# A graph network layer on one core: p from centred weights and the transposed accumulator, x loaded in 32x32 pieces, blocks in place of rows

## What is computed

```python
def reference(x, adj, L0_gnn_evals, L0_gnn_t, L1_gnn_W, L1_gnn_b):
    # L0: spectral filter
    t_eff = jnp.clip(t[0], 1e-08, None)
    x_spec = jnp.einsum('nk,nc->kc', adj, x)
    coefs = jnp.exp(-evals * t_eff)[:, None]
    out = jnp.einsum('nk,kc->nc', adj, coefs * x_spec)
    x = _layernorm(x + out, axis=-1)
    # L1: graph convolution
    adj_hat = adj + jnp.eye(N)
    deg = jnp.sum(adj_hat, axis=1, keepdims=True)
    out = (adj_hat / deg) @ (x @ W) + b
    return _layernorm(x + jnp.tanh(out), axis=-1)
```

## Time and profile before

| what | value |
|---|---|
| median of 3 runs (lowest, highest) | 615.78 us (615.32, 616.95) |
| the profiled execution, its own time | 615.71 us |
| its span, first to last instruction | 613.9 us |
| TensorE matmul busy | 579.9 us, 94% |
| VectorE busy | 511.1 us, 83% |
| ScalarE busy | 399.2 us, 65% |
| GpSimd busy | 378.2 us, 62% |
| moved by DMA | 174.67 MB, mean 285 GB/s |

### The profile page before, as it was taken

How to read it: one execution, slowest core, us unless ns; L and a number is a source line. 1 busy time by engine, 2 the same in 40 slices (tenths; PEclk the granted TensorE clock), 3 DMA queues, 4 the chain that set the end, 5 groups by cost and what they waited for, 6 DMA issues and landing times.

```text
span 613.9 us, 7999 instructions
## 1 busy us (share of the span) xinstructions
PE 579.9 (94%) x2460; PEld 447.1 (73%) x2460; DVE 511.1 (83%) x572; ACT 399.2 (65%) x855; POOL 378.2 (62%) x223
## 2 busy tenths in 40 slices
PE   5999999999998999989999999999999979899993
PEld 5888888888875656758888788887888856656561
DVE  4799999999898988888899799696776768989992
ACT  4999999999996746356555654555444635554552
POOL 0000000000147878788999999879887898997892
PEclk9999999999999999989999999999999999999997
DMA  8999999999999999799979999296995499999101
GB/s 306 408 409 408 410 408 409 409 410 407 410 271 346 328 330 341 212 259 269 242 209 260 254 305 272 66 256 192 256 258 142 123 342 347 348 339 316 35 18 52
DMA packets 125065, 174.67 MB, mean 285 GB/s; under 512 B 6884, under 2 KB 105700, under 8 KB 125032
## 3 DMA queue, kind: packets, MB, share of 16 engines
q1 hardware_dynamic: 72608, 121.68, 59.2%
q10 hardware_dynamic: 52424, 52.58, 30.6%
HBM read 172.13 MB, written 2.11 MB: 284 GB/s over the span
## 4 chain that ended last, share of the span: by engine, by line
PE 60%; POOL 22%; DVE 9%; DMA 3%; issue 3%; ACT 2%; ACTq 1%; DVEq 0%; POOLq 0%
POOL lo L483 18%; PE ps L833 9%; PE ps L835 9%; PE ps L834 9%; PE ps L861 8%; PE ps L863 8%; PE ps L862 8%; PE ps L857 7%; DVE vt L690 5%; DMA raw<-in_adj_dram 2%; DVE lo L697 2%; POOL rstd L462 2%; PE ps L818 1%; ACTq L368 1%; POOL raw L476 1%
## 5 line engine op out<-in xcount | busy, mean ns | idle before, releaser
L483 POOL TENSOR_TENSOR lo<-vt,hi 128x1024 fp32r<-128x1024 f32 x126 | 317.6, 2546 | 31.8 <-ACT hi L538 31.2
L690 DVE STREAM_TRANSPOSE vt<-raw 128x1024 f32<-128x1024 f32 x184 | 222.0, 1226 | 63.1 <-PE ps L863 52.1
L538 ACT ACTIVATE hi<-vt 128x1024 fp32r<-128x1024 f32 x159 | 165.8, 1060 | 128.6 <-DVE vt L690 104.6
L671 DVE TENSOR_TENSOR lo<-raw,hi 128x1024 fp32r<-128x1024 f32 x124 | 156.3, 1265 | 19.1 <-ACT hi L524 10.2
L524 ACT ACTIVATE hi<-raw 128x512 fp32r<-128x512 f32 x256 | 158.9, 623 | 7.2 <-PE ps L835 4.0
L436 POOL TENSOR_TENSOR lo<-raw,hi 128x1024 fp32r<-128x1024 f32 x4 | 10.2, 2556 | 170.7 <-ACT hi L524 170.7
L861 PE MATMUL ps<-hi,s_hi 128*128 128x512 f32 x224 | 94.5, 422 | 7.6 <-POOL lo L483 5.7
L833 PE MATMUL ps<-hi,xg_hi 128*128 128x512 f32 x256 | 100.2, 392 | 1.5 <-DVE lo L671 1.4
L834 PE MATMUL ps<-lo,xg_hi 128*128 128x512 f32 x256 | 99.6, 389 | 0.0
L835 PE MATMUL ps<-hi,xg_lo 128*128 128x512 f32 x256 | 99.6, 389 | 0.0
L861 PE MATMUL ps<-hi,p_hi 128*128 128x512 f32 x206 | 88.1, 428 | 6.9 <-POOL lo L483 6.9
(11 more groups left out here) (69 smaller groups left out, 537.5 us busy)
## 6 DMA issues: line engine op xcount, KB each, us to landing
raw<-in_adj_dram SPq DMA_DIRECT2D x63, 1024.0 KB, 14.3
raw<-in_adj_dram SPq DMA_DIRECT2D x90, 512.0 KB, 9.7
raw<-in_adj_dram ACTq DMA_DIRECT2D x88, 512.0 KB, 11.8
late_raw<-in_adj_dram SPq DMA_DIRECT2D x8, 512.0 KB, 12.6
late_raw<-in_adj_dram ACTq DMA_DIRECT2D x8, 512.0 KB, 14.5
xn<-in_x_dram SPq DMA_DIRECT2D x8, 256.0 KB, 14.0
x_sb<-in_x_dram SPq DMA_DIRECT2D x8, 256.0 KB, 13.7
out_dram<-x_sb ACTq DMA_DIRECT2D x7, 256.0 KB, 2.9
```

The source lines that it names most:

```text
L483: nc.gpsimd.tensor_tensor(lo[:, slot(p), :], vt[:, slot(p), :], hi[:, slot(p), :].bitcast(f32), ALU.subtract).then_inc(pool_lo_ready, 1)
L538: nc.scalar.activation(hi[:, slot(s), :], vt[:, slot(s), :], ACT.Copy).then_inc(hi_ready, 1)
L671: nc.vector.tensor_tensor(lo[:, q % RING1, :], raw[:, k, 2 * h:2 * h + 2, :].rearrange("p r n -> p (r n)"), hi[:, q % RING1, :].bitcast(f3 ...
L690: nc.vector.transpose(vt[:, slot(s), :].rearrange("p (m a i) -> p m a i", m=2, a=RB), load_buffer(st.load).rearrange("p (a m e i) -> p e m ...
```

## The change

1. **Weights.** `centre` = identity - 1/128 is made on GpSimd, TensorE multiplies it with W, and VectorE copies the result (V, W with each column's mean taken off) over `w_sb`, all ahead of stage 1. The transposes of the identity that nobody reads go from 36 to 20. TensorE now waits for W's load and for `centre` ahead of them, and VectorE for `centred` ahead of its first split of x.
2. **p.** Since layernorm only takes off the mean and scales, p = rstd * (h @ V). The ending becomes: since -3, VectorE turns x in 32x32 blocks into `stage[:, 1]`; since 0, VectorE adds it to acc2(g) into `stage[:, 0]` (h transposed), in place of ScalarE's copy; since 1, TensorE turns this (4); since 2, ScalarE copies h to x_sb; since 3, VectorE makes statistics, mean and variance together, and TensorE multiplies `stage[:, 0]` by V (4); since 6, ScalarE makes p_hi with the scale rstd, in four pieces; since 7, VectorE makes p_lo in four pieces; since 8, ScalarE normalises x_sb in place (x1) and makes `full`. The turning of x1 by TensorE and its copy by ScalarE are gone.
3. **x.** A group's x comes in four DMAs of 32 partitions, in pieces of 128 B, where it was one DMA in pieces of 2 KB.
4. **Blocks.** x_sb, 1/deg and the result are laid out in blocks as p is. The sums come back in four DMAs with pieces of 128 B, and VectorE turns them once. A result goes out in four DMAs a group, in pieces of 512 B, half of them issued by SyncE and half by ScalarE.

```diff
+    PHI = 6
-    x_v = x.rearrange("(u a e h r) c -> u e a h (r c)", u=NU, e=2, h=QP // R, r=R)
+    x_v = x.rearrange("(u a e i) (b c) -> u e b i a c", u=NU, e=2, i=QP, b=QN)
+    out_v = out.rearrange("(u q m e i) c -> u e m q i c", u=NU, q=QN, m=JB, e=2)
...
-                    sp.dma_start(x_sb[:, g, :], x_v[g // 2, g % 2]).then_inc(x_in[g % 2], 16)
+                    for b in range(QN):
+                        sp.dma_start(x_sb[b * QP:(b + 1) * QP, g, :].rearrange("i (a c) -> i a c", c=QP),
+                                     x_v[g // 2, g % 2, b]).then_inc(x_in[g % 2], 16)
...
             def ending2(g, since):
-                if since == 1:
-                    act.wait_ge(mm_done, END2[g] + 1)
-                    nc.scalar.activation(stage[:, 0, :], acc2(g), ACT.Copy).then_inc(acc_out, 1)
-                if since == 7:
-                    normalise(acc2(g), g % 2, g, g, rs2, x1_ready)
-                if since == 9:
-                    act.wait_ge(x1T_done, g + 1)
...
+                if since == 2:
+                    act.wait_ge(accT_done, g + 1)
+                    nc.scalar.activation(x_sb[:, g, :], acc2(g), ACT.Copy).then_inc(h_ready, 1)
+                if since == PHI:
+                    act.wait_ge(pw2, g + 1)
+                    act.wait_ge(hw_done, g + 1)
+                    for m in range(JB):
+                        last = nc.scalar.activation(p_hi[:, blocks(g, m)], acc2(g)[:, m * C:(m + 1) * C], ACT.Copy,
+                                                    scale=rstd[:, g % 2, m:m + 1])
+                    last.then_inc(phi_ready, 1)
+                if since == PHI + 2:
+                    normalise(x_sb[:, g, :], g % 2, g, g, rs2, x1_ready)
...
+            dve.wait_ge(centred, 1)
+            nc.vector.tensor_copy(w_sb[:, :], ps[:, NK - 2, :P]).then_inc(wc_ready, 1)
...
-                if since == 2:
-                    dve.wait_ge(accT_done, g + 1)
-                    dve.wait_ge(x_in[par], 16 * (g // 2 + 1))
-                    nc.vector.tensor_tensor(acc2(g), acc2(g), x_sb[:, g, :], ALU.add).then_inc(h_ready, 1)
+                if since == -3:
+                    dve.wait_ge(x_in[par], 16 * QN * (g // 2 + 1))
+                    nc.vector.transpose(stage[:, 1, :], x_sb[:, g, :]).then_inc(xT_ready, 1)
+                if since == 0:
+                    dve.wait_ge(mm_done, END2[g] + 1)
+                    dve.wait_ge(xT_ready, g + 1)
+                    if g:
+                        dve.wait_ge(hw_done, g)
+                    nc.vector.tensor_tensor(from_blocks(stage[:, 0, :]), by_block(acc2(g)), by_block(stage[:, 1, :]),
+                                            ALU.add).then_inc(hT_ready, 1)
...
-            for _ in range(36):
+            pe.wait_ge(w_in, 16)
+            pe.wait_ge(centre_ready, 1)
+            nc.tensor.matmul(ps[:, NK - 2, :P], centre[:, :], w_sb[:, :], start=True, stop=True).then_inc(centred, 1)
+            for _ in range(20):
                 nc.tensor.transpose(ps[:, NK - 1, :P], ident[:, :], ident[:, :])
             pe.wait_ge(coef_ready, 1)
+            pe.wait_ge(wc_ready, 1)
...
                 if since == 1:
-                    pe.wait_ge(acc_out, g + 1)
-                    for r in range(R):
-                        last = nc.tensor.transpose(acc2(g)[:, r * C:(r + 1) * C], spread(stage[:, 0, :], r), ident[:, :])
+                    pe.wait_ge(hT_ready, g + 1)
+                    for m in range(JB):
+                        last = nc.tensor.transpose(acc2(g)[:, m * C:(m + 1) * C], stage[:, 0, m * P:(m + 1) * P],
+                                                   ident[:, :])
                     last.then_inc(accT_done, 1)
-                if since == 8:
-                    pe.wait_ge(x1_ready, g + 1)
...
```

More of the change, by code:

```diff
@@ L246, in spectral_then_graph_conv @@
         ident = sb("ident", [P, P])
+        centre = sb("centre", [P, P])
         w_sb = sb("w_sb", [P, C])
@@ L303, in parts3, with blocks @@
             return [(range(R // 2), ps[:, bank, :], row + 1), (range(R // 2, R), ps[:, LATE3[0], :], row + 2)]
+        def blocks(g, m):
+            return slice((g * JB + m) * C, (g * JB + m + 1) * C)
         def columns(rows):
@@ L369, in load_quarters, with store @@
                               adj_q[ld.group // 2, ld.group % 2, ld.wide, q]).then_inc(block_in[ld.buf], 16)
+        def store(eng, row, count, odd):
+            g = ENDINGS[row]
+            for m in [ms for ms, _, n in parts3(row) if n == count][0][odd::2]:
+                eng.dma_start(out_v[g // 2, g % 2, m], x_sb[:, g, m * C:(m + 1) * C]).then_inc(stored, 16)
         blk = ctx.enter_context(nc.Block())
@@ L416, in _ @@
                     sp.wait_ge(deg_out, 16)
-                    for h in range(NG):
-                        sp.dma_start(rdeg[:, h, :], deg_by_group[h // 2, h % 2]).then_inc(deg_in, 16)
+                    for q in range(QN):
+                        sp.dma_start(rdeg_tile[q * QP:(q + 1) * QP].rearrange("p g r -> p (g r)"), deg_by_block[q])\
+                            .then_inc(deg_in, 16)
+            for row in range(NG):
+                for _, _, count in parts3(row):
+                    sp.wait_ge(out_ready, count)
+                    store(sp, row, count, 0)
         @blk.gpsimd
@@ L630, in ending3 @@
                         act.wait_ge(out_ready, count)
-                        act.dma_start(out_v[g // 2, g % 2][:, :, columns(rows_of)], x_sb[:, g, columns(rows_of)])\
-                            .then_inc(stored, 16)
+                        store(act, row, count, 1)
             for p in range(AHEAD, POSITIONS):
@@ L775, in ending3 @@
                 if since == 2:
-                    dve.wait_ge(deg_in, 16 * NG)
+                    if row == 0:
+                        dve.wait_ge(deg_in, 16 * QN)
+                        nc.vector.transpose(rdeg[:, :, :, :].rearrange("p u m e -> p (u m e)"),
+                                            rdeg_tile[:, :, :].rearrange("p g r -> p (g r)")).then_inc(deg_s, 1)
+                        dve.wait_ge(deg_s, 4)
                     for rows_of, bank, count in parts3(row):
@@ L932, in ending3 @@
                             pe.wait_ge(out_ready, ENDINGS.index(0) + 1)
-                        for r in rows_of:
-                            last = nc.tensor.transpose(bank[:, r * C:(r + 1) * C], spread(stage[:, row % 2, :], r),
+                        for m in rows_of:
+                            last = nc.tensor.transpose(bank[:, m * C:(m + 1) * C], stage[:, row % 2, m * P:(m + 1) * P],
                                                        ident[:, :])
                         last.then_inc(sumT_done, 1)
-            pe.wait_ge(w_in, 16)
             for p in range(AHEAD, POSITIONS):
```

77 lines of the change are left out of this document (41 added, 36 removed).

## The result

| | before | after |
|---|---|---|
| median (lowest, highest), 6 runs each | 616.37 us (613.65, 618.59) | 631.86 us (628.36, 632.24) |
| ratio, with its 95% interval | | 1.0245 (1.022 to 1.0271) |
| span of the profiled execution | 613.9 us | 630.2 us |
| x alone undone (runs below; before 615.53 us in these) | | 620.48 us |
| x and the stores undone | | 611.59 us |

The change makes the kernel slower by 15.5 us. The forecast was 611.2 us with a range to 617.5: wrong in its sign. What it said of two kinds of DMA, x in pieces of 128 B (+1.7) and the stores (-0.1), was wrong by some 10 and 9 us.

A forecast was written before the change was run, and what follows sets the result against it. TensorE was taken as the bound, except from 285 to 348 us, where GpSimd's subtractions set the pace. Ten terms from -1.65 to +1.7 summed to -4.5, so 615.7 became 611.2 us, range 606.5 to 617.5.

The forecast's parts named there:

- x in pieces of 128 B: Group 0: small pieces make SyncE's queue 7.7 us later, load 4 lands at 218.4, GpSimd's chain starts 1.65 later: +1.7.
- in group 1 ... VectorE's and GpSimd's slack there covers: Group 1: SyncE's queue is late again by some 2 to 3 us at load 8, covered by slack.
- Later groups: 0: Groups after 1: 7.7 us more of queue time just fits, or the sums' return saves 4.6 us: 0.
- The end: Last results go out on two queues, and the sums come back in 128 pieces for 1024: -0.1 us.
- The start: Stage 1: with 20 transposes for 36, the first matmul comes at about 12.9 for 14.06, and this lasts: -1.15 us.
- Addition ahead of the transposes: Group endings: TensorE's transposes wait for VectorE's addition, 2.0 us in group 1, 0.9 in group 5, 0.2 in group 0.
- Mean and variance, the pause, the clock: Group 1: mean and variance 1.0 us earlier, pause before step 40 shrinks, clock stays up: about -1.65.
- the clock in the 4 us behind the new wait: Behind TensorE's new wait in group 1: clock at 1.00 means the forecast, at 0.5 rival C, 1.3 more.
- rival C: Chance 0.20: clock falls in group 1 (+1.3), VectorE's work costs up to 1, half-clock stays at group 7 (+0.7): 614.2 us.
- p, the other groups, VectorE's 8.4 us "hidden": VectorE's added 8.4 us costs 0; groups 0: -0.9, 3: +0.1, 4: -0.4, 5: -0.4, 6: -0.5, 7: -1.2.
- D: Chance 0.11: SyncE's queue becomes the bound; at 120 ns a pair load 4 lands at 222.5, x costs +13: 622.5 us.
- E: Chance 0.04: each small piece of x is done twice, two passes of 88 ns, 22.5 us a group: 639.5 us.

The follow-up runs named there:

- b3: The changed kernel with x of groups 0 and 1 loaded by GpSimd's queue in stage 1 and all stores issued by SyncE: 612.46 us.
- a1: The changed kernel with each group's x loaded as before, in one DMA with pieces of 2 KB: 620.48 us.
- a4: The changed kernel with x of groups 0 and 1 loaded by GpSimd's queue in stage 1, in the same 128 B pieces: 620.73 us.
- f1: d3 with 36 transposes of the identity again in place of 20: 611.99 us.
- d3: b3 with VectorE's addition written ahead of the lo subtraction of its position, in the two groups that have one: 610.74 us.
- a3: a1 with the stores as before too, one DMA a row in pieces of 2 KB, all on ScalarE: 611.59 us.
- a2: The kernel before the change with only x changed, to four DMAs a group in pieces of 128 B: 630.98 us.
- d2: The changed kernel with all stores on SyncE and each of a group's four x DMAs issued behind another of its loads: 633.26 us.
- b1: a1 with all 32 stores issued by SyncE, in the same pieces: 612.32 us.

## Why the prediction was wrong, point by point

- **x in pieces of 128 B, +1.7: measured +11.4.** This is the first step that failed. It took the price from pieces of 16 B in the earlier trace rows, at most 88 ns a pair, 11.3 us for x0. The 2048 pieces of x0 took 16.2 us, 127 ns for each of an engine's 128, those of x1 15.5. And it asked only how late SyncE's queue would be, though all queues share the engines: in these stretches they moved 3295 and 2943 pieces of 1 KB where b3 moves 5490 and 5270. Load 4 then came for a turn at 222.35, not 218.4; x0 costs 10.0 us at step 16, measured against a1's turn. The next step of the argument, "in group 1 ... VectorE's and GpSimd's slack there covers", fell with it: the distance to a1 grows to 14.2 by step 32. How the 10.0 us divide between the engines' time and x standing ahead of load 4 in SyncE's queue is open. "Later groups: 0" was right (a4).
- **The end, -0.1: measured +8.9.** The second step that failed, and not even in the range. (The profiles say 7.0.) It counted bytes and pieces, and left out that ScalarE issues: what stands in its queue behind a store is its own loads, and behind those, on the engine, hi and `stage` of the next steps.
- **The start, -1.15.** The first product came at 12.82 as forecast (12.9), the first turn of stage 2 1.2 earlier in the changed kernel's profile. f1 doesn't confirm that this lasts.
- **Addition ahead of the transposes.** Waits of 2.37 in group 1 (2.0), 0.47 in group 5 (0.9), 1.37 in group 0 (0.2, there with loads late). That the wait was on the path is shown by d3, in its trace more than in its median, whose ratio's interval overlaps b3's.
- **Mean and variance, the pause, the clock.** Right for the pause: none before step 40, and 1.88 for 3.20. By the prediction's own sign, the clock in the 4 us behind the new wait, the changed kernel is rival C's case (0.50, as above) and a3 the forecast's (1.00). In a3 the turns from step 36 to 50 go from +0.5 to -4.3 against before, of which 1.9 are given back by step 62: more than the 1.65 forecast.
- **p, the other groups, VectorE's 8.4 us "hidden".** All terms but x and the end came to -6.1, and a3 measured -3.9. In its trace steps 16 to 36 lose 1.5 us (from -1.0 to +0.5) where group 0 was to gain 0.9. Group 5 gains 1.2 for 0.4 (from -3.1 in steps 82 to 88 to -4.4 in 120 to 126). At group 7 the -7.1 of step 152 are -3.2 at step 164; a2, whose endings are the old ones, shows a dip of 2.7 and then a loss of 1.9 at the same steps, so neither is shown to be the new ending's. The half-clock stretch there stayed as long, as rival C had it: 0.50 for 3.4 us, from 504.8 us in the kernel before and from 498.4 in a3. VectorE's busy time grew by 10.3 us. Which of its new pieces costs the time in group 0 was not tried.
- **Rivals.** D, held at 0.11, comes nearest. From 120 ns a pair it had x0 take 15.4 us and load 4 land at 222.5, with x at +13; measured are 16.2 us, a turn at 222.35 and +11.4. Its 622.5 us lack the stores. But the lateness of one queue is not all of it: d2 takes SyncE's burst away and gets slower. E read two passes for each small piece out of the Trainium skill's page "DMA: Bandwidth & Descriptors", Specifications, which says that below 512 B an engine does read-modify-write. The count gives 1.1 pieces of 1 KB for one of 128 B and 1.2 to 1.4 for one of 512 B: no second pass, and no dearer piece below 512 B, shows in these runs.

The parts, -3.9 + 11.4 + 8.9 = 16.4 us, are differences between one run and the next, so they add up by their making; that the two kernels measured 15.5 apart is due to before, 616.37 us there and 615.53 beside a1 and a3. That the two losses are separate is shown by the stores alone: moved to SyncE they give back 8.2 us with x in 2 KB pieces (a1, b1) and 8.3 with x early (a4, b3).

## What to carry to other kernels

Read the DMA engines' share and their GB/s at the very place where a transfer moves, not over the span: the share was 1.10 at 347 GB/s and 1.13 at 202. Where all queues have loads to bring and compute needs them at once, a new piece is taken from the loads of all queues, and slack in lateness on the one queue says nothing. Count small pieces by number, and put them where no engine waits for the loads beside them: the same 2048 pieces cost 10.0 us in group 0 and 4.2 more in group 1 (turns against a1's) and nothing later. A DMA belongs on a queue whose engine has nothing on the path behind it; moving 16 stores from ScalarE to SyncE was worth 8 us without touching a byte.

## What the runs showed of the hardware that was not expected

- Pieces of 128 B beside 1 KB loads took the place of 1.1 of these each, 51 to 54 ns against 47, while their own recorded time on the queue was low (SyncE's queue 37.4% with 2963 packets, ScalarE's 76.3% with 2550). Pieces of 512 B took that of 1.2 to 1.4.
- One queue alone moved 202 GB/s of 1 KB pieces at a share of 1.13, both together 348.
- Issuing DMAs is no constant. A load's DMA of 512 pieces took as little as 0.42 us on SyncE ahead of x0, and 3.0 on average in the eight behind it. At one place two of them on ScalarE took 0.92 with no store ahead, 5.21 behind two stores of 128 pieces and 6.30 behind one of 512; elsewhere in b1 two take up to 3.13 without any store.
- Spreading the same small pieces evenly between the loads was worse than a burst behind each group's last load (633.26 us, against 612.46 with them out of the way).
